# Last cross attention: the value products of two units issued together, in the first and third quarter of the step

## What is computed

```python
q = (x @ Wq).reshape(B, Sq, h, d).transpose(0, 2, 1, 3)          # 8 heads, d = 64
k = (context @ Wk)...;  v = (context @ Wv)...                    # 375 keys
attn = softmax(einsum('bhid,bhjd->bhij', q, k) * d ** -0.5)
out = einsum('bhij,bhjd->bhid', attn, v) -> (B, Sq, 512) @ Wo + bo
x = x + out
x = x + (mx_quantize(x) @ mx_quantize(weight).T + bias)
```

## Time and profile before

| | us |
|---|---|
| median of 3 executions | 2233.82 |
| lowest, highest | 2224.35, 2236.61 |
| the profiled execution, device time | 2225.22 |
| its span in the trace | 2223.4 |
| PE busy in the span | 2050.3 (92%) |
| DVE, ACT, POOL busy | 1412.7, 1035.3, 891.6 |

### The profile page before, as it was taken

How to read it: one execution, slowest core, us unless ns; L and a number is a source line. 1 busy time by engine, 2 the same in 40 slices (tenths; PEclk the granted TensorE clock), 3 DMA queues, 4 the chain that set the end, 5 groups by cost and what they waited for, 6 DMA issues and landing times. The chain is left out here.

```text
span 2223.4 us, 61979 instructions
## 1 busy us (share of the span) xinstructions
PE 2050.3 (92%) x21235; PEld 1670.6 (75%) x21236; DVE 1412.7 (64%) x3682; ACT 1035.3 (47%) x2466; POOL 891.6 (40%) x1479
## 2 busy tenths in 40 slices
PE   5999999999879999959999999959999999999996
PEld 4777777777657777748999999947777777777774
DVE  4666667666448888854333233226787887878785
ACT  2444444444334444423233233226666666666663
POOL 3444444444136666640000000025656566666651
PEclk9999999999889999979999999969999999999998
DMA  6222232225050000021111111120111111101010
GB/s 183 80 77 77 79 96 83 77 77 202 2 164 18 25 21 21 23 77 32 35 35 38 36 35 38 35 86 21 36 30 35 30 35 30 37 28 39 26 29 9
DMA packets 98790, 118.81 MB, mean 53 GB/s; under 512 B 9778, under 2 KB 91442, under 8 KB 98610
## 3 DMA queue, kind: packets, MB, share of 16 engines
q1 hardware_dynamic: 92594, 103.43, 15.3%
q0 software_dynamic: 6144, 14.69, 2.2%
HBM read 67.36 MB, written 50.72 MB: 53 GB/s over the span
## 5 line engine op out<-in xcount | busy, mean ns | idle before, releaser
L1263 ACT ACTIVATE e_act_T<-ps_quad,fc_b 128x128 f32<-128x128 f32 x504 | 136.8, 383 | 313.3 <-PE ps_quad L1328 313.3
L479 DVE TENSOR_REDUCE a_negmax<-ps_turned 112x2 f32<-112x750 f32 x256 | 240.0, 938 | 59.8 <-PE ps_turned L569 58.5
L1328 PEld LDWEIGHTS ps_quad<-e_xT,e_w_now 128*128 128x128 f32 x2016 | 236.6, 193 | 7.9 <-DVE e_xT L1297 4.1
L1328 PE MATMUL ps_quad<-e_xT,e_w_now 128*128 128x128 f32 x2016 | 237.6, 276 | 3.5 <-DVE e_xT L1297 3.5
L422 ACT ACTIVATE a_probsT<-ps_quad 125x896 f32<-125x896 f32 x192 | 176.2, 918 | 128.0 <-PE ps_quad L581 123.7
L1343 PE MATMUL ps_out<-w,e_act_T 128*128 x1008 | 228.1, 379 | 0.8 <-DVE e_y L1305 0.8
L1441 POOL COPY c_index<-slot 112x1 uint32 (+1 forms) x64 | 19.4, 332 | 477.8 <-POOLq L1226 477.8
L1343 PEld LDWEIGHTS ps_out<-w,e_act_T 128*128 128x128 f32 x1008 | 186.6, 190 | 24.0 <-issue 1.2
L1294 DVE COPY e_w_now<-w 128x2048 f32 x63 | 77.3, 1227 | 200.4 <-PE ps_quad L1328 190.5
L1468 POOL TENSOR_TENSOR c_kL<-c_kT,c_kH 128x376 fp32r<-128x376 f32 x128 | 126.5, 988 | 169.3 <-ACT c_kH L1520 168.7
L206 ACT ACTIVATE c_probs<-ps_quad,c_negmax 112x375 f32<-112x375 f32 x256 | 144.0, 571 | 26.8 <-DVE c_negmax L167 26.8
(11 more groups left out here) (304 smaller groups left out, 5287.5 us busy)
## 6 DMA issues: line engine op xcount, KB each, us to landing
slots<-a_zeros SPq DMA_DIRECT2D x60, 512.0 KB, 5.0
a_cT<-in_ctx_t SPq DMA_DIRECT2D x32, 375.0 KB, 3.6
c_cT<-in_ctx_t SPq DMA_DIRECT2D x32, 375.0 KB, 3.2
w<-in_fc_t SPq DMA_DIRECT2D x2, 4096.0 KB, 21.7
w<-in_fc_t SPq DMA_DIRECT2D x8, 1024.0 KB, 11.8
e_xg<-slots SPq DMA_DIRECT2D x63, 128.0 KB, 2.0
slots<-e_y SPq DMA_DIRECT2D x63, 128.0 KB, 1.7
out<-c_fo SPq DMA_DIRECT2D x32, 112.0 KB, 1.9
```

Source lines behind the costliest of these rows:

```text
L479: dve.tensor_reduce(negmax[:, t, e, :].rearrange("p (r c) -> p r c", c=32)[:, 2 * half:2 * half + 2, 0], plain[0:T, :, 0:CTX], AX, ALU.max ...
L1263: last = act.activation(act_T[par][:, c * TILE:(c + 1) * TILE], hidden[par][:, c // 4, (c % 4) * TILE:(c % 4 + 1) * TILE], ACT.Gelu, bias= ...
L1328: last = pe.matmul(hidden[par][:, c // 4, (c % 4) * TILE:(c % 4 + 1) * TILE], w1_now[:, k, c * 128:(c + 1) * 128], xT[par][:, k, :], start ...
```

## The change

The value products of a batch are no longer issued one unit per quarter, three quarters behind. Those of units 0 and 1 come together in quarter 0 of the next step, those of units 2 and 3 together in its quarter 2. `probsT` has four buffers in place of two, and ACT's spread waits for the value products of four units back. ACT's copy `oT` moves from quarter 2 to quarter 3, behind the spread and ahead of `qT`.

```diff
-        self.probsT = [sb(f"probsT{i}", [chunk, heads, self.chunks, T]) for i in range(2)]
+        self.probsT = [sb(f"probsT{i}", [chunk, heads, self.chunks, T]) for i in range(4)]
...
-                                 v(u, j, c), self.probsT[u % 2][:, j, c, :],
+                                 v(u, j, c), self.probsT[u % 4][:, j, c, :],
...
-        return self.probsT[u % 2][:, :, :, :].rearrange("p h c t -> p h (c t)"), self.turned[u % len(self.turned)]
+        return self.probsT[u % 4][:, :, :, :].rearrange("p h c t -> p h (c t)"), self.turned[u % len(self.turned)]
...
-            wait(act, self.values_ready, n - 1)
+            wait(act, self.values_ready, n - 3)
...
-                        if u == 2 and exists(b - 1):
+                        if u == 3 and exists(b - 1):
                             act.wait_ge(core.values_ready, b * U)
                             wait(act, op_mm, b - 1)
                             act.activation(oT[:, :, :].rearrange("p k t -> p (k t)"), psum["out"][:, 0:4 * T], ACT.Copy)\
...
-                        at = core.behind(b, u, core.VALUE)
-                        if exists(at[0]):
-                            if u == 3:
-                                pe.wait_ge(v_ready, 3 * b + 3)
-                                wait(pe, o_ready, b)
-                            core.pe_values(pe, *at, v_of(par if u >= 3 else 1 - par))
+                        if u in (0, 2) and exists(b - 1):
+                            if u == 0:
+                                pe.wait_ge(v_ready, 3 * b)
+                                wait(pe, o_ready, b - 1)
+                            core.pe_values(pe, b - 1, u, v_of(1 - par))
+                            core.pe_values(pe, b - 1, u + 1, v_of(1 - par))
```

## The result

| | before | after |
|---|---|---|
| median, executions on one chip (13 each) | 2235.04 us | 2243.68 us |
| lowest, highest | 2224.35, 2240.1 | 2238.88, 2251.4 |
| ratio after / before, 95% interval | | 1.0053 [1.0034, 1.0071] |
| profiled execution, its span | 2225.22, 2223.4 | 2243.68, 2241.8 |

The change costs about half a per cent: 0.0053 x 2235 is 11.8 us, with bounds of 7.6 and 15.9. The forecast was 11.2 us more and 2241.

What follows compares the result with a forecast made beforehand. PE's matmuls bound the kernel, busy 21.49 of 21.71 us in an odd step. The loop's 14 x (0.35 + 0.26) = 8.5 plus 2.7 for the ends gave +11.2 us, forecast 2241; likeliest case 2234 to 2249, 8 in 10 2227 to 2254.

Steps and rivals of the forecast that it cites:

- V in quarter 3 was free: Between Q and OP: V lay inside OP's wait for `qT`, so moving it away gains 0.02 us instead of 0.73.
- The wait that was announced as 15 to 20 us: OP's matmuls would newly wait for ACT's `c_qT`, about 0.5 to 0.7 us in each of 28 steps.
- The rival in which OP does not stay pinned: OP not held 2.59 behind Q; saved drains and covered stall count in full, 19 us faster; chance 0.07.
- Quarter 0, a second V 0.59; covered in the even step, 0.36 net in the odd: Unit 0's V added before value projection 0: K3 starts +0.00 later in even steps, 0.36 us in odd ones.
- Quarter 1, -0.67: Without V, scores come sooner, but the key product waits for projection 1's copy: 0.67 us gained, 0.05 lost to a wait.
- Quarter 2, +0.59: Unit 3's V joins unit 2's and adds 0.59 us; the copy of projection 2 stays hidden.
- The collision in the even step, +0.43: Between steps, POOL's earlier `c_kL` holds DVE's `c_xd` (L1191): XD +0.32 us on PE, `qT` another 0.1 late.
- In the odd step [...] some 0.15 after L1191's start; whoever starts first has it, so no cost.: Between odd steps, POOL's `c_kL` comes 0.32 us earlier yet still behind DVE's L1191, so no collision.
- rival 3: More waits: odd steps collide too, or `oT` makes `qT` late in all steps; +17 us, 2247; chance 0.17.
- The ends, +2.7: Outside the loop: step 1 +0.5 us, step 30 +0.3, step 31 with its tail +1.9, steps 32 and 33 none.
- The rule on the change of tiling mode: Trainium skill: changing tiling mode drains TensorE; pairing V would then save two drains a step, 0.14 us each.
- 8.5 us forecast for the loop: 14 pairs of steps, even +0.35 and odd +0.26 us each, the even step's collision included.

Runs made afterwards that it cites:

- cut_q3: Kernel before with the value product of quarter 3 cut from 12 matmuls to 4 in steps 1 to 31; 2229.53 us, before 2232.19 on the same chip.
- pair_q0: Only unit 0's V moved, from quarter 3 to quarter 0, against the kernel before, `oT` in quarter 2; 2233.32 us, before 2230.59 on the same chip.
- kl_after_xd: Changed kernel with POOL's `c_kL` of tile 0 made to wait for DVE's `c_xd`; 2238.25 us, before 2230.59 on the same chip.
- pair_q2: Only units 2 and 3 paired in quarter 2, against the kernel before, `oT` in quarter 2; 2224.86 us, before 2223.49 on the same chip.
- pair_q2_xd: pair_q2 with POOL's `c_kL` of tile 0 made to wait for DVE's `c_xd`; 2219.27 us, before 2223.49 on the same chip.
- copy_before: Kernel before, unchanged, profiled a second time; 2222.27 us in a single execution.
- ot_back: Changed kernel with ACT's copy `oT` put back in quarter 2; 2239.94 us, before 2230.59 on the same chip.

## Why the prediction was right, and where it was not

The sign, the size (+11.2 against +11.8) and the mechanism came as forecast; one step of it was wrong (the odd step's collision) and one term too small (the end of the stage). The total is closer than its parts, and that is in part luck: by the first profile of before, on which the sum was made, the stage and step 1 cost 17.8.

- **V in quarter 3 was free** (term -0.02). Right: 2.61 to 2.62 between Q and OP in after, 2.58 in cut_q3 and pair_q0. The wait that was announced as 15 to 20 us came as 19.3. The rival in which OP does not stay pinned fell with it.
- **Quarter 0, a second V 0.59; covered in the even step, 0.36 net in the odd.** Measured 0.57, +0.03 and +0.33. Right for steps 3 to 29; pair_q0 shows it alone. Step 2 has no stall to cover, which the sum left out: +0.57 there.
- **Quarter 1, -0.67.** Measured -0.60. Key product 0 starts 0.83 to 0.84 behind the scores, not 0.76: the new short wait for the copy was 0.13, not 0.05.
- **Quarter 2, +0.59.** Measured +0.57.
- **The collision in the even step, +0.43.** L1191 at 1.19, XD held: right. Its price by kl_after_xd is 0.31 rather than 0.43: XD is held 0.26 and not 0.32, and OP comes 2.62 behind Q where kl_after_xd has 2.58, 0.04 rather than 0.1. DVE as a whole lost little by it: the normalisation behind `c_xd` (L178) no longer has `c_kL` beside it and takes 0.74 where it took 1.55. The even step is +0.30 against +0.35.
- **"In the odd step [...] some 0.15 after L1191's start; whoever starts first has it, so no cost."** This step failed. `c_kL` starts 0.11 ahead of L1191 there (1844.34, 1844.45), and kl_after_xd takes back 0.36. I had moved only `c_kL` and left L1191 at its old place in the step. It is later too: 14.75 behind the step's first scores (1829.70), where it was 14.41 (1823.96). The trace has the delay in quarter 1, on POOL and DVE; odd step before, then after:

```profile
1830.51 0.98 POOL L1468 TENSOR_TENSOR c_kL<-c_kT,c_kH 128x376 fp32r<-128x376 f32 x1 [1.99 <-ACT c_kH L1520]
1830.82 1.21 DVE L178 TENSOR_SCALAR c_probs<-c_probs,c_recip 112x375 f32<-112x375 f32 x2
```

```profile
1836.58 0.98 POOL L1468 TENSOR_TENSOR c_kL<-c_kT,c_kH 128x376 fp32r<-128x376 f32 x1 [2.30 <-ACT c_kH L1520]
1836.64 1.45 DVE L178 TENSOR_SCALAR c_probs<-c_probs,c_recip 112x375 f32<-112x375 f32 x2
```

The second V in quarter 0 delays value projection 0, and with it on ACT the copy `c_v` and `c_kH` behind it; so POOL's `c_kL` of key tile 2 starts 6.88 behind the first scores in place of 6.55. The normalisation L178 beside it ends 0.53 to 0.54 behind the end of `c_kL` both times, so 0.32 later, and what follows on DVE up to L1191 keeps that. The runs bear it out: in the odd steps of every kernel with a second V in quarter 0 L178 takes 1.45 to 1.46 there and L1191 starts 14.73 or more behind the first scores; in those of pair_q2 and pair_q2_xd it takes 1.20 to 1.21 and L1191 starts at 14.42 to 14.45. The part of rival 3 on the odd step, with a chance of 0.17, is what happened. The odd step is +0.61 against +0.26: 14 x 0.35 is 4.9 us.
- **The ends, +2.7.** Step 1 is 0.45 longer from its first scores to OP (20.73 against 20.28; forecast 0.5), step 30 0.22 (0.3), steps 31 and 32 3.8 (1.9). The sum had OP of step 31 late by 1.4, and 0.5 for the rest of the two steps; it came 2.1 late behind the step's first scores (17.87 against 15.74), and its matmuls then ran at the lower clock, 3.40 against 1.98, which the sum did not have: 1.42 of the 1.9 that are missing. (From the last OP, that of step 32, on PE runs at the lower clock in eleven of the twelve profiles, whatever the kernel, 3.16 for its eight matmuls in the second profile of before and 1.89 in the first; the end from there, 21.3 to 23.7, is therefore not set against the change.)
- **The rule on the change of tiling mode.** A switch around V costs 0.14 in the trace, as the forecast had it, and pairing takes one away at each V: 1.30 rather than 1.46. But pair_q2_xd, where one pair is formed and all waits but that of key product 0 are as before, gains 0.01 to 0.03 a step. The saving of 0.16 goes where V left quarter 1, into the wait for the projection's copy (0.13). That the 0.14 is the change of mode, and not something else at the border of two groups, no run here shows.

With 8.5 us forecast for the loop and 13.3 found against the first profile of before (11.3 against the second), and ends of 2.7 forecast and 4.5 found (4.3), the trace gives +17.8 or +15.6 in place of +11.2; the interval of the ratio, 7.6 to 15.9, holds the second of the two. The 2.0 us in the loop between the two profiles of before lie at the one place named under copy_before, which appears in kernels with and without moved value products. Why the timed ratio, +11.8, comes out nearer the forecast than either stays open.

## What to carry to other kernels

Before moving work away from a place on the busiest engine, ask what that engine would do there without it: between Q and OP the PSUM bank was waiting for a copy, so the work was free, and each place it can go to has a price. When an instruction moves earlier, move its neighbours on the other engines with it, in every kind of step, and look for each pair of DVE and POOL instructions whose starts are a few tenths of a us apart. A forecast lead of 0.15 us was no lead here. And a wait that a change could cover may be better traced to its cause: here the same 11.3 us of stall went by moving one call on POOL, for 12.5 us gained [7.8, 17.4].

## What the runs showed of the hardware

- A DVE instruction with two tensors in SBUF that began just behind or within a tensor-tensor of POOL ended 0.28 to 0.29 behind POOL's end, whatever its own length: 0.43 became 1.16 to 1.19 (L1191, 0.08 to 0.11 behind POOL's start), 0.41 became 1.24 (residual add), and two that took 1.09 together took 2.34 beside two of POOL that took 2.11 (L1590). L178, a tensor-scalar with one tensor in SBUF, was held as well: 0.74 for two where POOL was idle, 1.21 and 1.45 beside `c_kL`, 1.55 behind `c_xd` in before. `c_o` and `c_f` (L1632, L1636), with one of their inputs in PSUM, took their 0.41 to 0.42 beside `c_cL`. An instruction of DVE that looks two or three times as long as its own shape elsewhere may be a waiting one, and no row of the waits tells so.
- After PE had been busy 0.18 of 2.40 us, the next eight matmuls took 3.40 at a granted clock of 0.54, against 1.98 at 1.00. The clock was still 1.00 in the idle stretch itself, so the price of a wait can appear behind it. With the wait gone (ot_back) the same matmuls took 1.89.
